# Loading the far pieces of an adjacency matrix as 32-partition transfers instead of 128-partition transfers

## The reference

```python
h = jnp.maximum(_layernorm(x, axis=-1), 0.0)
A_hat = adj + jnp.eye(adj.shape[0], dtype=adj.dtype)
d_inv_sqrt = jnp.sum(A_hat, axis=1) ** (-0.5)
A_norm = d_inv_sqrt[:, None] * A_hat * d_inv_sqrt[None, :]
out = x + jax.nn.relu(A_norm @ (h @ W.T))
```

## Time and profile before

| | |
|---|---|
| three timed runs | 1187.28, 1252.42, 1238.79 us; median 1238.79 us |
| the profiled execution's own time | 1192.53 us |
| its span, first to last instruction | 1190.7 us |
| mean granted TensorE clock | 0.918 of full speed |
| busy: TensorE, VectorE, ScalarE | 82%, 68%, 49% of the span |
| moved by DMA | 381.32 MB, mean 320 GB/s |

### The profile page before, as it was taken

One profiled execution on the slowest core, in us unless ns is written; L12 is line 12 of the kernel. 1 busy time (PEld: TensorE's weight loads), 2 busy tenths in 40 slices (PEclk: granted clock), 3 DMA queues, 4 the chain that ended last, 5 costly groups with the idle time before them and its releaser, 6 DMA issues.

```text
span 1190.7 us, 9309 instructions
## 1 busy us (share of the span) xinstructions
PE 979.3 (82%) x2363; PEld 448.5 (38%) x2363; DVE 813.2 (68%) x969; ACT 578.5 (49%) x1719; POOL 128.7 (11%) x102
## 2 busy tenths in 40 slices
PE   0634356668489797989979999999999899899997
PEld 0631122223234243434434444444444344344443
DVE  5442244456467576767868788888888788687785
ACT  2898685776565646362635625215436552110011
POOL 3121021020110101010000101001001000010011
PEclk9876667789789898989989999999999999999999
DMA  9899999999999999999999999999999959999994
GB/s 297 309 360 383 390 397 362 367 384 349 357 362 335 361 333 341 329 336 304 328 281 363 277 338 329 336 300 296 319 305 267 324 156 284 290 266 316 330 331 116
DMA packets 266628, 381.32 MB, mean 320 GB/s; under 512 B 10448, under 2 KB 246096, under 8 KB 266576
## 3 DMA queue, kind: packets, MB, share of 16 engines
q1 hardware_dynamic: 133360, 190.40, 51.2%
q10 hardware_dynamic: 133216, 190.34, 51.0%
HBM read 376.50 MB, written 4.19 MB: 320 GB/s over the span
## 4 chain that ended last, share of the span: by engine, by line
PE 43%; DMA 3%; ACT 2%; DVE 2%; ACTq 1%; issue 1%; POOLq 0%; SPq 0%; DVEq 0%
PE bank L502 42%; DMA slot<-in_adj_dram 3%; ACT junk L550 2%; DVE adjT L698 1%; DVE part L682 1%; ACTq L286 1%; PE pre L478 0%; ACT slot L540 0%; ACTq L294 0%; DVE kept_cell L783 0%; ACT kept_cell L568 0%; POOLq L187 0%; PE sums_bank L466 0%; ACTq L328 0%; SPq L286 0%
## 5 line engine op out<-in xcount | busy, mean ns | idle before, releaser
L502 PE MATMUL bank<-adjT,support 128*128 128x512 f32 x2048 | 934.2, 617 | 115.7 <-DVE adjT L698 110.6
L698 DVE STREAM_TRANSPOSE adjT<-slot 128x1024 f32<-128x1024 f32 x430 | 521.6, 1232 | 206.2 <-PE bank L502 102.0
L502 PEld LDWEIGHTS bank<-adjT,support 128*128 128x128 f32 x2048 | 401.3, 198 | 626.7 <-issue 622.8
L550 ACT ACTIVATE junk<-slot 128x384 bf16<-128x384 f32 (+2 forms) x732 | 348.1, 477 | 255.3 <-issue 197.0
L540 ACT ACTIVATE slot<-slot 128x6144 f32<-128x6144 f32 (+11 forms) x56 | 166.4, 2971 | 159.5 <-issue 85.0
L550 ACT ACTIVATION_READ_ACCUMULATOR junk<-slot 128x1 f32 x732 | 136.6, 187 | 0.0
L422 POOL COPY kept_cell<-slot 128x2048 f32<-128x2048 f32 x35 | 65.1, 1892 | 593.4 <-DMA slot<-in_adj_dram 475.3
L568 ACT ACTIVATE kept_cell<-kept_cell,dinv 128x128 f32<-128x128 f32 x64 | 20.2, 389 | 173.1 <-DVE kept_cell L792 68.4
L698 DVE STREAM_TRANSPOSE adjT<-kept_cell 128x1024 f32<-128x1024 f32 x70 | 85.6, 1235 | 26.5 <-PE bank L502 26.5
L682 DVE TENSOR_REDUCE part<-slot 128x4 f32<-128x1536 f32 (+2 forms) x61 | 94.3, 1561 | 8.9 <-DMA slot<-in_adj_dram 8.9
L466 PE MATMUL sums_bank<-by_block,spread 128*128 128x64 f32 x32 | 7.5, 326 | 45.6 <-DVE by_block L733 45.6
(11 more groups left out here) (53 smaller groups left out, 181.3 us busy)
## 6 DMA issues: line engine op xcount, KB each, us to landing
slot<-in_adj_dram ACTq DMA_DIRECT2D x134, 768.0 KB, 13.6
slot<-in_adj_dram SPq DMA_DIRECT2D x134, 768.0 KB, 15.4
slot<-in_adj_dram ACTq DMA_DIRECT2D x66, 512.0 KB, 12.7
slot<-in_adj_dram SPq DMA_DIRECT2D x66, 512.0 KB, 13.7
slot<-in_adj_dram ACTq DMA_DIRECT2D x8, 1536.0 KB, 15.7
slot<-in_adj_dram SPq DMA_DIRECT2D x8, 1536.0 KB, 16.0
slot<-in_adj_dram ACTq DMA_DIRECT2D x4, 1408.0 KB, 17.0
slot<-in_adj_dram SPq DMA_DIRECT2D x4, 1408.0 KB, 17.9
```

Of the source, the lines that this page charges most:

```text
L502: ins = nc.tensor.matmul(bank[bank_of(g)][:], support[:, v * R + t, :], adjT[at % TURNS][:, r, :], start=(n == first_of[g] and t == 0), st ...
L550: nc.scalar.activation(junk[at % JUNKS][:, :n], cells[:, c, :], ACT.Copy, accum_out=part[u % 2][:, k, c:c + 1]).then_inc(junk_done, 1)
L698: nc.vector.transpose(adjT[at % TURNS][:].rearrange("p t (c i) -> p t c i", i=Q), half.rearrange("p c (t r) -> p t c r", r=Q)).then_inc(t_ ...
```

## The change

`load_far` no longer gives each queue all 128 partitions and two of the four column quarters. It gives each queue half of the partitions and all four quarters, in transfers of 32 partitions: SyncE's queue takes partitions 0 to 31 and 32 to 63, ScalarE's 64 to 95 and 96 to 127. The length and the number of the contiguous runs stay the same, as do the bytes of each queue. The number of far DMAs goes from 56 to 112 on each queue, each with 128 runs instead of 256. `landed` counts four DMAs for each row block instead of two.

```diff
-        landed.append(16 * sum(2 * landing[k][3] if landing[k][0] == "far" else B for k in earlier + [m]))
+        landed.append(16 * sum(B * landing[k][3] if landing[k][0] == "far" else B for k in earlier + [m]))
...
             to = far_block(m).rearrange("p a (b j) -> p a b j", b=B)
-            b0 = quarters[0]
-            for a in range(n):
-                queue.dma_start(to[:, a, b0:b0 + 2, :],
-                                adj_far[u, :, bb + a, b0:b0 + 2, v * CELL:(v + cells) * CELL]
-                                ).then_inc(ld_slot[slot_of[m]], 16)
+            for k in quarters:
+                p = slice(k * Q, (k + 1) * Q)
+                for a in range(n):
+                    queue.dma_start(to[p, a, :, :],
+                                    adj_far[u, p, bb + a, :, v * CELL:(v + cells) * CELL]
+                                    ).then_inc(ld_slot[slot_of[m]], 16)
```

## The result

| | before | after |
|---|---|---|
| median of 20 runs | 1253.08 us | 1259.65 us |
| lowest to highest | 1187.28 to 1285.55 us | 1248.15 to 1267.69 us |
| profiled execution: time, span | 1192.53, 1190.7 us | 1257.71, 1255.9 us |

The ratio after to before is 1.0554, 95% interval 1.048 to 1.0627: slower. It compares the undisturbed runs of each kernel, those near its lowest; the runs of the kernel before are spread over 8% and those of the changed one over 1.6%, which is why the medians lie so close and the ratio doesn't. The profiled executions lie 5 us above the lowest run of the kernel before and 10 us above that of the changed one; their spans are 65 us apart.

A forecast was written before the change was run, and what follows sets the result against it. Transfers were taken to bound the kernel up to about 601 us, TensorE's matmuls after. Terms of -22 + 3 + 1 + 2 = -16 us took 1238.79 to 1223 us (1176.5 at the profile's level); range 1160 to 1260 us.

The forecast's parts named there:

- What bounds the kernel: Whole span: transfer rate sets the time ahead of about 601 us, TensorE's matmuls the 590 us after.
- Term 2: Far plateaus: long runs in the 32-partition shape are about 2% slower; 3 us lost, bounds 0 to 5.
- Term 1: Passages between cells and far pieces: unlike shapes cause the dips, one shape removes them; 22 us gained, bounds 0 to 30.
- Term 3: At the start, ScalarE's queue alone in one half of the partitions is held to 232 GB/s; 1 us lost.
- Term 4: Issue of twice as many far DMAs: hidden beside transfers except at stripe 12's far piece; 2 us lost.
- C: Far pieces: queues fall out of step, each held to its half; at 25% of bytes net +29 us; chance 0.12.
- D: Far pieces: queues writing disjoint halves serialize at 232 GB/s; about 1358 or 1404 us; chance 0.03.
- B: Passages: dips come from switching between pieces of any shape and remain; +6 us, 1198 or 1245; chance 0.18.
- The level: Whole execution: the runs' median lies 46 us above the profile; the forecast was given at the median's level, 1238.79 us.

The follow-up runs named there:

- e8: Kernel before, with far pieces in 64-partition, four-quarter transfers in stripes 7 to 12 only, number of DMAs unchanged: median 1185.79 us, ratio 0.9947.
- e1: Kernel before, with far pieces still to 128 partitions but one column quarter for each DMA, 112 on each queue: median 1216.26 us.
- e7: Changed kernel, with one far DMA of 64 partitions and four quarters for each queue and row block, 56 on each queue: median 1244.57 us, ratio 1.0424.
- e4: Changed kernel, with most long far runs cut to 1024 or 1536 bytes, same bytes, DMAs and partitions: median 1220.76 us.
- b1: Kernel before, unchanged, run against itself: median 1249.35 us, runs 1193.36 to 1257.92; its profiled execution took 1241.72 us.
- e6: Changed kernel, with SyncE's queue on partitions 0-31 and 64-95, ScalarE's on 32-63 and 96-127: median 1319.42 us, ratio 1.1139 to the kernel before.
- e2: Changed kernel's destination of 32 partitions, but each far DMA reads 128 rows of one quarter: 1252.06 us.
- e3: Changed kernel's source of 32 rows and four quarters, but written to all 128 partitions: 1209.12 us.

## Why the prediction was wrong

**What bounds the kernel: right.** Transfers set the time up to about 600 us. The 66 us lost by stripe 7 are 65 at the end, with 9 won and 8 lost in between.

**Term 2 failed, and decided the case.** I drew a line through cells of 1024 and 1536 bytes and read off 239 ns, 411 GB/s, for a 6144-byte run in the 32-partition shape, a loss of 0 to 5 us. Measured: 292 GB/s in stripe 0 and 264 in stripe 1. Worked out from the bytes of each stripe and its two rates, 405 to 418 GB/s before and 264 to 321 after, stripes 0 to 6 lose about 13, 18, 13, 10, 8, 6 and 5 us, 73 us in all. The lag itself grew by 13, 15, 15, 9, 7, 5 and 1 us, 66.5 in all. That the shorter dips give back the difference is likely, but not measured by itself. The step that failed is the extrapolation over a factor of four in run length: the trace of before had no long run to few partitions, and this term's bound should have reached to the nearest such row however far, the 232 GB/s of one queue alone. I used that row only for a queue out of step. The row that I thought settled it, stripe 10 at 372 in the 128-partition shape, is a stretch of 2 us, and it says only that the shapes are equal at 1536 bytes.

**Term 1: mechanism right in part, size too large.** With far pieces dealt as cells are, the dips on the way in vanish and those on the way out shrink, but after stripes 9 and 10 they still last 8 and 6 us. That there is "nothing unlike left to meet" was too strong: the dip at 601 us stands between pieces of one shape, and only their run lengths differ, 1536 and 1024 bytes. Whether that makes it, no run tests. e8, where little else changes, is worth 9 us at stripe 11, nearly all of it won in stripes 9 and 10, and the changed kernel made up the same 9 us between stripes 7 and 11. Against 22 us forecast: the early meetings can't be had without their stripes' long runs, part of the late ones remains, and part of the gain is paid back in the plateau (3072-byte runs at 339 GB/s in e8 for 399 before).

**Term 3: direction right, mis-sized.** I expected 1 us at the start. The effect I had priced was there: from 16 to 24 us ScalarE's queue moved 1.65 MB instead of 2.08, 206 GB/s, so the same bytes take 10 us instead of 8. But stripe 1 began 12.9 us late. By e1 some 3.8 of it is the number of DMAs; by e7, 9.4 us come without any more DMAs, from stripe 0's far pieces on the slow plateau.

**Term 4: mis-sized.** I expected 0.36 us for an issue of 128 runs. The issuing instructions of the changed kernel:

```profile
L295 ACTq DMA_DIRECT2D slot<-in_adj_dram x112: 567/621/1648, 9.7 to 736.3; - x112
```

They take 0.62 us, more than one of 256 runs did, and e1's, also of 128 runs, take 0.45. So the pattern of the transfer costs, not just its runs; which feature of it does is open, since e4's uncut stripe 2, also 128 runs to 32 partitions, takes 0.41. I said that transfers cover it; at the start none does, and e1's lowest run is 19 us up, where I had counted 2 us. How much of the 65 us this is in the changed kernel I can't separate, since a slow plateau also covers more issues; e7, with half the issues and slightly better plateaus, is 15 us below it.

**The rivals.** C had the right direction and the wrong mechanism: it asked for queues out of step. In the 46 us at 264 GB/s SyncE's queue moved 6.29 MB and ScalarE's 5.87. D, that halves on two queues serialize, is wrong as stated: 264 to 345 GB/s is above 232, and cells keep 370. The warning that the Trainium skill gives beside it ("DMA: Bandwidth & Descriptors", "Rules for kernel authors": use one 128-partition transfer) pointed the right way for long runs. B, that the dips come from switching between pieces of whatever shape and remain, is wrong for the passages into far pieces and right in part for those out of them. Its price left the plateaus alone.

**The level.** 46 us between the profile and the median of the runs shown looked like something to add to both kernels. b1 shows that the kernel before has it by itself, in the one upper run that I profiled as a low rate that lasts through stripes 7 to 10. The changed kernel's runs hardly spread, which fits unlike shapes as the cause; it isn't shown, and e6, with 32-partition transfers throughout, spreads by 4% in four runs. I should have kept the profile's level for the lower end and left the median open. The measured median of 1259.65 us lies inside my range only because that range ran up to the highest run plus B's 6 us: that was luck, since it is the plateaus that make the kernel slower, and term 2 had put them at 3 us.

**What stays open.** Why long runs to half of the partitions are slow is shown by its conditions only (destination, e2 and e3; run length, e4; halves, e6 and e7). The port map that the Trainium skill gives in "SBUF — State Buffer", "Door 1: The DMA port swizzle", gives each half of the partitions its own eight ports. By it e6 puts both queues on the same eight, which agrees with 237 against 345 GB/s and 227 against 292; no row shows a port. That a long run holds a port longer against another engine is only a guess of mine. Why stripe 0 has 292 and stripe 1 264 at the same run length is open too. So is what starts and ends the lasting low rate in the kernel before, and what makes the dips that the changed kernel keeps.

## What to carry to other kernels

A transfer rate holds for its shape and its run length together; before reading one off a line, ask whether the trace holds a row with both, and if not, let the bound reach to the nearest row that has one of them. Where transfers of two shapes follow each other, look at the rate in slices of 1 us around the passage, and at how much the kernel's runs spread, since the kernel that is slower at best can be the steadier one, as here. A change that gains in some stages and loses in others is worth splitting by stage: here changing only the late stripes kept the gain, half a per cent.

## What the runs showed of the hardware

- Transfers to half of the partitions, one half for each queue: 368 GB/s with 1536-byte runs, 345 with 3072, 316 with 3584, 302 with 4608, 276 with 5632, and 292 and 264 with 6144 (stripes 0 and 1). To all 128 partitions: 413 with 4608, 418 with 6144.
- Both queues moving between the halves, 3072-byte runs: 237 GB/s instead of 345; 6144-byte runs in stripe 0: 227 instead of 292.
- Issue time of a DMA of 128 runs on ScalarE's queue: 0.45 us with 128 partitions and one run in each, 0.62 us with 32 partitions and four. In e4's stripe 2, also with 32 partitions and four, it is 0.41 us.
- After a passage between the two shapes a low rate, 244 to 276 GB/s, lasted for some 65 us in one execution and for 3 to 12 us (up to 552 us) in another of the same program.
- Between two pieces of the same shape, with 1536 and 1024-byte runs, a dip can occur too: 222 GB/s for 6 us from 601 us of the changed kernel, which has 346 to 351 right after it.
